# Where the weights are split: from GpSimd to ScalarE and VectorE, in a fused AdaLN block with linear attention and routed experts

## The chip, the cores and the metric

The kernel runs on one NeuronCore of a Trainium2 chip. The metric is the device time of one execution in microseconds (us). The kernel before was timed three times: 1975.85, 1978.46 and 1978.96 us, median 1978.46. The page and the trace come from one more, profiled execution.

## What is computed

x is 4096 tokens (2 sequences of 2048) by 512, all in float32. Cut to what matters, with `_rms`, `_layernorm`, `_silu` and `gelu` as usual:

```
sa, ca, ga, sb, cb, gb = (_silu(c) @ wmod)            # six rows per sequence; ga, gb kept away from zero
h = _layernorm(x) * (1 + ca) + sa
q, k, v = split(_rms(h) @ w_qkv.T);  q = _rms(q);  k = _rms(k);  w = exp(k)
y = sigmoid(q) * (cumsum(w * v) / (cumsum(w) + 1e-6))  # along the sequence
u, g = split(y @ w_swiglu.T)
x = x + ga * (h + u * silu(g) @ w_out.T)               # DFF = 2048
h = _layernorm(x) * (1 + cb) + sb
routed = top 2 of 8 experts of gelu(h @ w1 + b1) @ w2 + b2, softmax gates, H = 256
shared = gelu(h @ shared_w1 + shared_b1) @ shared_w2 + shared_b2
x = x + gb * (routed + shared)
```

## The kernel before

It is written by hand, engine by engine: five instruction streams (`@block.sync` for the DMA queue SP, `gpsimd`, `tensor`, `scalar`, `vector`), each executed in the order in which it is written, tied together by semaphores. A `wait_ge` holds all that stands behind it on its engine.

Every large product is float32 in three passes: an operand is held as a high part (`fp32r`) and a low part (the rest), and TensorE adds hi·hi, hi·lo and lo·hi (`product` L685 to L688, `by_tokens` L690 to L693). So each weight, too, is fetched raw and split once: a copy that rounds (hi), then a subtraction raw - hi (lo). The weights come in 36 pieces, numbered in the order of use: pieces 0 to 3 are w_qkv, split in six halves on ScalarE and VectorE (`weights_hi`, `weights_lo`); B0 = 4 to 11 and C0 = 12 to 19 are the two halves of the first feed-forward, 128x1536 each; S0 = 20 to 23 the shared expert's and R0 = 24 to 39 the routed experts', 128x1024 each. Pieces 4 to 39 are split by GpSimd in `split_piece` (L548 to L559) and fetched into two raw buffers in turn: pieces 4 to 7 by SP (`piece`), the others by GpSimd (`fetch`). `w_ok` counts pieces that are done. TensorE waits for it ahead of the first use of each; a piece takes the place of one that is no longer read, hence the waits on `dn` ahead of the splits.

The stages, in the words used below:

- **Stage A**, 32 groups of 128 tokens. For each group g TensorE does k (12 products), turns the next group's rows, `turn_group` (L720), then q (12 products), turns the last group's w, e and w·v (`sums`: L750, L754, L761), then v (12 products). VectorE does in the same loop (L1536 to L1558): `k_times_v(g-1)` (L1459), `quotient(g-2)` (L1501 to L1503), in every fourth group `roots` and `deviations`, then `columns_lo(g+1)` (L1434, which TensorE's next group waits for), `scales(g)` (L1442 to L1450, which wait for squares from ScalarE), `denominator(g-1)` (four scans, L1474, and L1478), `sum_kv(g-1)` (four scans, L1489), and `norm(g+4)` (L1406, L1417).
- **Stages b and c**, the first feed-forward in two passes over 8 tiles of 512 tokens. A tile has 8 blocks s: 24 products up (L686 to L688) and, two blocks later, 12 down (L691 to L693). ScalarE does silu (L1183) and hi (L1185) of a block, VectorE the product `s_t` (L1567) and lo (L1570); then VectorE has its hooks: in b, `token_stats` at s = 2 and `first_residual` (L1616 to L1620) at s = 3 to 6, in c the second norm and the router. After a tile come `x_lo` of the next (L1354, which TensorE waits for) and `evacuate` (L1629, L1633). TensorE can go up two blocks beyond the last block that VectorE has finished.
- **Stage s**, the shared expert, 8 tiles of 4 blocks; its low part is L1843. Between the blocks VectorE does the router of the last two tiles (`positions`, L1689 to L1703) and the tables of the experts.
- **Stage r**, 71 slots of 128 gathered rows, each through one expert. GpSimd gathers rows (L632) and adds results to `out` (L642). Ahead of the first slots VectorE finishes the last shared tile: `last_shared`, then `last_residual` (L1909) for four row groups, after which SP stores the tile, and `slot_o(0)` waits for that store (`out_st`) before it writes the first `o_t` (L1935).

GpSimd's order around the splits: pieces 4 to 7 in stage A, 8 to 11 from A's end on, 12 to 19 as b's last tile frees the places, then the router's writes (`to_lists`, L597) in turn with 20 to 35, the first gathers, 36 and 37, more gathers, 38 and 39.

Of the kernel before, what the change touches and what calls it, by code (L numbers as in the profile page):

```python
# [34 lines left out]
def build(nc, x_tok, c, wmod, w_qkv, w_swi, w_sh, w_exp, b1s, b1r, b2p, b2s, gate_w, ident, tri, rank, tokid, ebase,  # L35
# [48 lines left out]
    with ctx:  # L84
# [238 lines left out]
        def _(sp):  # L323
            def piece(i):

                sp.wait_ge(w_ok, max(i - 1, B0))
                src, _, _, n = piece_of(i)
                sp.dma_start(raw[i % 2][:, 0:n], src).then_inc(raw_in[i % 2], 16)

# [217 lines left out]
        def _(pool):  # L547
            def split_piece(i):  # L548
                _, hi, lo, n = piece_of(i)
                if i < SP_PIECES:  # L550
                    pool.wait_ge(raw_in[i % 2], 16 * (i // 2 - 1))
                else:
                    pool.wait_ge(raw_sw[i % 2], 16 * ((i - SP_PIECES) // 2 + 1))
                src = raw[i % 2][:, 0:n] if i < S0 else raw_4[i % 2][:, :]
                if i >= R0:
                    src = src.rearrange("p (m n) -> p m n", n=hi.shape[2])
                nc.gpsimd.tensor_scalar(hi, src, 1.0, 1.0, ALU.mult, ALU.mult).then_inc(w_hi_ok, 1)  # L557
                pool.wait_ge(w_hi_ok, i + 1)
                nc.gpsimd.tensor_tensor(lo, src, hi.bitcast(F32), ALU.subtract).then_inc(w_ok, 1)  # L559

            def fetch(i):
                pool.wait_ge(w_ok, i - 1)
                src, _, _, n = piece_of(i)
                pool.dma_start(raw[i % 2][:, 0:n] if i < S0 else raw_4[i % 2][:, :], src).then_inc(raw_sw[i % 2], 16)


            pool.wait_ge(w_ok, B0)
            for i in range(B0, B0 + 2):
                split_piece(i)

            split_piece(6)
            fetch(8)
            split_piece(7)
            fetch(9)
            pool.wait_ge(a.mm, 3 * NG)
            for i in range(8, C0):
                split_piece(i)
                fetch(i + 2)
# [6 lines left out]

            for j in range(NB):
                pool.wait_ge(ffn["b"].dn, NB * LAST + j + 1)
                split_piece(C0 + j)
                fetch(C0 + j + 2)
# [13 lines left out]
            for j, freed in enumerate((0, 1, 2, 2)):  # L603
                pool.wait_ge(ffn["c"].dn, NB * LAST + freed + 1)
                split_piece(S0 + j)
                fetch(S0 + j + 2)

            for i in range(R0, R0 + 4):
                pool.wait_ge(ffn["c"].dn, NB * LAST + (5 if i < R0 + 2 else 6))
                split_piece(i)  # L610
                fetch(i + 2)
# [1 line left out]
            for i in range(R0 + 4, R0 + 8):
                pool.wait_ge(ffn["c"].dn, NB * NT)
                split_piece(i)
                fetch(i + 2)

            pool.wait_ge(hT_st, 16 * NT)
            pool.wait_ge(n2.logit_mm, NT)
            pool.wait_ge(hr_st, 16 * NSUB * NT)  # L620
# [1416 lines left out]
```

## Time and profile before

| | |
|---|---|
| three runs, us | 1975.85, 1978.46, 1978.96 |
| the profiled execution, us | 1976.18 |
| its span in the trace, us | 1974.1 |
| TensorE busy | 97% |
| VectorE, ScalarE, GpSimd busy | 67%, 34%, 23% |
| TensorE's mean granted clock | 0.989 of full |
| tile period in b | 65.28 us |
| group period in A, undisturbed | 10.0 us |

The busy share of TensorE (PE) counts a product from issue to its modelled end, so neighbours overlap; what counts are the gaps, and the stretches at a lower granted clock. PEld is its weight load, DVE VectorE, ACT ScalarE, POOL GpSimd. Times are microseconds from the span's start. A line of the timeline has start, duration, engine, line, operation, tiles, shapes and count, and in brackets how long the engine had been idle and what ended that.

### The profile page before, as it was taken

Reading aid. Unit: us, or ns where it says so; the run is one execution under the profiler, and the core shown is the slowest. Engines: PE = TensorE matmul, PEld = TensorE weight load, DVE = VectorE, ACT = ScalarE, POOL = GpSimd, SP = SyncE. Lnnn points to the kernel's source line nnn. Section 1 sums busy time; section 2 is a strip of 40 time slices with the busy share of each in tenths; the row PEclk is TensorE's granted clock in tenths of the full one; section 3 lists DMA queues with packets and bytes.
Section 4 is the critical chain, followed back from the end, with each engine's and each line's share of the span. In section 5 each row is a group of like instructions: output and inputs, shape, how many; then the busy total and the mean of one; then the engine's idle time right before and its main releaser. Section 6 shows DMA issues by size and latency. Waiting matters only on the chain.

```text
span 1974.1 us, 26317 instructions
## 1 busy us (share of the span) xinstructions
PE 1915.7 (97%) x8850; PEld 1536.1 (78%) x8850; DVE 1315.2 (67%) x2728; ACT 665.5 (34%) x1376; POOL 444.2 (23%) x319
## 2 busy tenths in 40 slices
PE   6998999999999999998999999999999989899998
PEld 4677888878888888886887787787786767688886
DVE  5789999875545554567256356456458587488887
ACT  4666776421112111111112212212223333255554
POOL 0031000220000000035001011011062351588885
PEclk9999999999999999998999999999999999999999
DMA  5224110231110211034011321311234464488887
GB/s 187 99 91 142 54 54 27 68 116 65 64 45 21 75 64 53 12 112 155 22 65 54 98 66 59 114 67 59 93 119 170 141 193 156 147 155 154 154 153 107
DMA packets 86686, 189.96 MB, mean 96 GB/s; under 512 B 9525, under 2 KB 26198, under 8 KB 81516
## 3 DMA queue, kind: packets, MB, share of 16 engines
q1 hardware_dynamic: 63564, 130.92, 19.7%
q0 software_dynamic: 22992, 57.37, 14.0%
q8 instruction: 74, 1.21, 0.3%
q14 instruction: 56, 0.46, 0.1%
HBM read 118.56 MB, written 72.12 MB: 97 GB/s over the span
## 4 chain that ended last, share of the span: by engine, by line
PE 66%; DVE 8%; POOL 3%; issue 3%; ACT 1%; DMA 1%; POOLq 0%; DVEq 0%
PE bank L686 12%; PE bank L688 11%; PE bank L687 11%; PE bank L691 7%; PE bank L692 6%; PE bank L693 6%; PE bank L929 3%; POOL out L642 1%; PE bank L856 1%; PE bank L931 1%; PE bank L959 1%; PE bank L958 1%; PE bank L957 1%; PE bank L916 1%; POOL rows_t L632 1%
## 5 line engine op out<-in xcount | busy, mean ns | idle before, releaser
L686 PE MATMUL bank<-x_hi,w_blk 128*128 128x512 f32 x1024 | 404.5, 395 | 9.2 <-DVE x_lo L1354 5.4
L688 PE MATMUL bank<-x_hi,w_blk 128*128 128x512 f32 x1024 | 400.1, 391 | 0.0
L687 PE MATMUL bank<-x_lo,w_blk 128*128 128x512 f32 x1024 | 399.5, 390 | 0.0
L1567 DVE TENSOR_TENSOR s_t<-act_t,bank 128x512 f32<-128x512 f32 x128 | 87.8, 686 | 305.3 <-PE bank L688 305.0
L1185 ACT ACTIVATE s_hi<-s_t 128x512 fp32r<-128x512 f32 x128 | 80.9, 632 | 458.1 <-DVE s_t L1567 458.1
L686 PEld LDWEIGHTS bank<-x_hi,w_blk 128*128 128x128 f32 x1024 | 192.9, 188 | 51.4 <-DVE x_lo L1354 6.6
L688 PEld LDWEIGHTS bank<-x_hi,w_blk 128*128 128x128 f32 x1024 | 192.8, 188 | 40.9
L687 PEld LDWEIGHTS bank<-x_lo,w_blk 128*128 128x128 f32 x1024 | 193.1, 189 | 38.8
L557 POOL TENSOR_SCALAR w_blk<-raw 128x1536 fp32r<-128x1536 f32 x16 | 24.2, 1514 | 814.3 <-PE bank L693 663.6
L691 PE MATMUL bank<-w_blk,s_hi 128*128 128x512 f32 x512 | 200.7, 392 | 0.0
L693 PE MATMUL bank<-w_blk,s_lo 128*128 128x512 f32 x512 | 199.4, 389 | 0.0
L692 PE MATMUL bank<-w_blk,s_hi 128*128 128x512 f32 x512 | 199.3, 389 | 0.0
L1183 ACT ACTIVATE act_t<-bank 128x512 f32<-128x512 f32 x128 | 76.3, 596 | 354.5 <-PE bank L688 354.5
L597 POOL DMA_INDIRECT slot_list<-pay,pos x64 | 64.2, 1003 | 557.5 <-DVE pos L1703 540.1
L691 PE MATMUL bank<-w_blk,xc_hi 128*128 128x512 f32 x384 | 158.5, 413 | 6.0 <-DVE xc_lo L1434 4.8
L1570 DVE TENSOR_TENSOR s_lo<-s_t,s_hi 128x512 fp32r<-128x512 f32 x128 | 92.3, 721 | 89.5 <-ACT s_hi L1185 88.8
L693 PE MATMUL bank<-w_blk,xc_lo 128*128 128x512 f32 x384 | 151.7, 395 | 0.0
L692 PE MATMUL bank<-w_blk,xc_hi 128*128 128x512 f32 x384 | 151.0, 393 | 0.0
L642 POOL DMA_INDIRECT out<-o_t,ids_t x71 | 113.9, 1604 | 31.9 <-DVE o_t L1935 28.9
L691 PEld LDWEIGHTS bank<-w_blk,s_hi 128*128 128x128 f32 x512 | 96.1, 188 | 25.7 <-issue 6.2
L929 PE MATMUL bank<-w_all,xT_hi 128*128 x284 | 110.5, 422 | 5.3 <-issue 5.3
L693 PEld LDWEIGHTS bank<-w_blk,s_lo 128*128 128x128 f32 x512 | 96.1, 188 | 20.2
(264 smaller groups left out, 3637.5 us busy)
## 6 DMA issues: line engine op xcount, KB each, us to landing
x_t<-y_scratch SPq DMA_DIRECT2D x24, 1024.0 KB, 4.8
residual<-r_t SPq DMA_DIRECT2D x16, 1024.0 KB, 4.3
r_t<-residual SPq DMA_DIRECT2D x16, 1024.0 KB, 5.7
raw<-w_swi POOLq DMA_DIRECT2D x12, 768.0 KB, 4.6
y_scratch<-y_t SPq DMA_DIRECT2D x32, 256.0 KB, 2.6
r_t<-x_tok SPq DMA_DIRECT2D x8, 1024.0 KB, 5.3
h_rows<-hrow SPq DMA_DIRECT2D x32, 256.0 KB
y_scratch<-hT SPq DMA_DIRECT2D x8, 1024.0 KB, 3.9
```

Source lines behind the costliest of these rows:

```text
L642: pool.indirect_dma_start(out, bass.IndirectOffsetOnAxis(ap=ids_t[:, j:j + 1], axis=0), o_t[j % NO][:, :], None, compute_op=ALU.add).then_ ...
L686: nc.tensor.matmul(dst, w[:, 0, col:col + P], rhs_hi, start=start, stop=False)
L687: nc.tensor.matmul(dst, w[:, 0, col:col + P], rhs_lo, start=False, stop=False)
L688: return nc.tensor.matmul(dst, w[:, 1, col:col + P], rhs_hi, start=False, stop=stop)
L691: nc.tensor.matmul(dst, lhs_hi, w[:, 0, col:col + D], start=start, stop=False)
L692: nc.tensor.matmul(dst, lhs_hi, w[:, 1, col:col + D], start=False, stop=False)
L693: return nc.tensor.matmul(dst, lhs_lo, w[:, 0, col:col + D], start=False, stop=stop)
L929: nc.tensor.matmul(bank_u[j % 2][:, 0:2 * H], xT_hi[:, j % 2, tok], w_all[:, bass.ds(at_e + m * 2 * H, 2 * H)], start=(m == 0), stop=False)
L1183: nc.scalar.activation(act_t[:, s % 2, :], bank[4 + 2 * s % 3][:, :], ACT.Silu).then_inc(f.act_ok, 1)
L1185: nc.scalar.activation(s_hi[:, s % 3, :], s_t[:, s % 2, :], ACT.Copy).then_inc(f.sh_ok, 1)
L1567: nc.vector.tensor_tensor(s_t[:, s % 2, :], act_t[:, s % 2, :], bank[4 + (2 * s + 1) % 3][:, :], ALU.mult).then_inc(f.s_ok, 1)
L1570: nc.vector.tensor_tensor(s_lo[:, s % 3, :], s_t[:, s % 2, :], s_hi[:, s % 3, :].bitcast(F32), ALU.subtract).then_inc(f.sl_ok, 1)
```

## The change

GpSimd splits nothing any more; it only fetches, all 36 pieces. `piece_hi` is a copy on ScalarE, `piece_lo` the subtraction on VectorE, both placed by hand: pieces 4 to 7 in groups 8, 12, 16 and 20 of stage A; 8 to 11 in blocks 0 to 3 of b's first tile; 12 to 16 in blocks 3 to 7 of b's last tile, 17 to 19 in blocks 0 to 2 of c's first; 20 to 23 in blocks 3 to 6 of c's last; twelve in stage s (`S_TURNS`), two in its last block, two in slots 1 and 3. Two orders change beside that: `sums_kv` now stands behind the v products, and `sum_kv` a group later and ahead of `quotient`; and the last three `last_residual` stand behind the first slots' work.

```diff
-        late_rows = [o_t[4], o_t[5], p_t[0], p_t[1]]
+        late_rows = [p_t[0], p_t[1], o_t[4], o_t[5]]
...
+        def pieces_at(p, t, s):
+            if p == "b" and t == 0 and s < 4:
+                return (B0 + 4 + s,)
+            if p == "b" and t == LAST and s >= 3:
+                return (C0 + s - 3,)
+            if p == "c" and t == 0 and s < 3:
+                return (C0 + 5 + s,)
+            if p == "c" and t == LAST and 3 <= s < 7:
+                return (S0 + s - 3,)
+            if p == "s" and (t, s) == (LAST, 3):
+                return (R0 + 12, R0 + 13)
+            if p == "s" and (t, s) in S_TURNS:
+                return (R0 + S_TURNS.index((t, s)),)
+            return ()
+
+        S_TURNS = ((1, 1), (1, 2), (1, 3), (2, 1), (2, 3), (3, 0), (3, 2), (3, 3), (4, 2), (4, 3), (5, 0), (5, 2))
+
+        A_TURNS, R_TURNS = (8, 12, 16, 20), (1, 3)
...
-            if t == 5:
+            if t == 4:
                     gates_out(LAST)
...
-            def split_piece(i):
...
             def fetch(i):
-                pool.wait_ge(w_ok, i - 1)
...
+                pool.wait_ge(w_ok, max(i - 1, B0))
+                pool.dma_start(raw_of(i)[:, 0:piece_of(i)[3]], piece_of(i)[0]).then_inc(raw_sw[i % 2], 16)
...
                 ins.then_inc(a.cum, 1)
+
+            def sums_kv(g):
                 pe.wait_ge(a.kv_ok, g + 1)
...
                     sums(g - 1)
                 project(g, 2)
+                sums_kv(g - 1)
...
+            def piece_hi(i):
+
+                src, hi, _, n = piece_of(i)
+                act.wait_ge(raw_sw[i % 2], 16 * ((i - B0) // 2 + 1))
+                act.wait_ge(w_ok, max(i - 1, B0))
...
+                nc.scalar.activation(hi, from_, ACT.Copy).then_inc(w_hi_ok, 1)
...
+                if g in A_TURNS:
+                    piece_hi(B0 + A_TURNS.index(g))
...
+                        for i in pieces_at(p, t, s):
+                            piece_hi(i)
...
                 slot_o(j)
+                if j in R_TURNS:
+                    piece_hi(R0 + 14 + R_TURNS.index(j))
...
+            def piece_lo(i):
+
+                _, hi, lo, n = piece_of(i)
+                dve.wait_ge(w_hi_ok, i + 1)
...
+                nc.vector.tensor_tensor(lo, from_, hi.bitcast(F32), ALU.subtract).then_inc(w_ok, 1)
...
                 if g >= 2:
+                    sum_kv(g - 2)
                     quotient(g - 2)
...
                 denominator(g - 1)
-                sum_kv(g - 1)
...
                     norm(g + NSUB)
+                if g in A_TURNS:
+                    piece_lo(B0 + A_TURNS.index(g))
...
+                        for i in pieces_at(p, t, s):
+                            piece_lo(i)
...
             last_residual(0)
             slot_g(0)
-            for g in range(1, NSUB):
-                last_residual(g)
             for j in range(NSLOT):
...
                     slot_g(j + 1)
+                if j == 0:
+                    for g in range(1, NSUB):
+                        last_residual(g)
+                if j in R_TURNS:
+                    piece_lo(R0 + 14 + R_TURNS.index(j))
```

VectorE at the end of group 8 of stage A, before (rk_a ends `scales`; xr is `norm`, kv_t `k_times_v` of the next turn of the loop):

```order
L1450 SCALAR_TENSOR_TENSOR rk_a<-b_a,y_a 128x2
L1474 SCALAR_TENSOR_TENSOR W_t_55<-bank,W_t_54,tri_t 128x128 x4
L1478 SCALAR_TENSOR_TENSOR den_t_59<-bank,W_t_55 128x512
L1489 SCALAR_TENSOR_TENSOR kv_sum_57<-bank,kv_sum_56,tri_t 128x128 x4
L1391 TENSOR_TENSOR sqv<-sv_a 128x4
L1392 SCALAR_TENSOR_TENSOR sqv<-sqv,va_a 128x4
L1393 SCALAR_TENSOR_TENSOR rs_a<-sqv,sv_a 128x4
L1406 SCALAR_TENSOR_TENSOR xr<-xr,mv_a,gain_a_93 128x512
L1417 SCALAR_TENSOR_TENSOR xr<-xr,rs_a,shift_a_95 128x512
L1459 SCALAR_TENSOR_TENSOR kv_t_66<-bank,r_pair,w_t_64 128x512
L1501 TENSOR_TENSOR den_t_59<-den_t_59,rec_t 128x512
```

and of the change:

```order
L1469 SCALAR_TENSOR_TENSOR rk_a<-b_a,y_a 128x2
L1493 SCALAR_TENSOR_TENSOR W_t_55<-bank,W_t_54,tri_t 128x128 x4
L1497 SCALAR_TENSOR_TENSOR den_t_59<-bank,W_t_55 128x512
L1410 TENSOR_TENSOR sqv<-sv_a 128x4
L1411 SCALAR_TENSOR_TENSOR sqv<-sqv,va_a 128x4
L1412 SCALAR_TENSOR_TENSOR rs_a<-sqv,sv_a 128x4
L1425 SCALAR_TENSOR_TENSOR xr<-xr,mv_a,gain_a_93 128x512
L1436 SCALAR_TENSOR_TENSOR xr<-xr,rs_a,shift_a_95 128x512
L1383 TENSOR_TENSOR w_blk<-raw_83,w_blk 128x1536
L1478 SCALAR_TENSOR_TENSOR kv_t_66<-bank,r_pair,w_t_64 128x512
L1508 SCALAR_TENSOR_TENSOR kv_sum_57<-bank,kv_sum_56,tri_t 128x128 x4
L1520 TENSOR_TENSOR den_t_59<-den_t_59,rec_t 128x512
```

The four scans of kv_sum have moved behind the next kv_t, and the subtraction of piece 4 stands between the norm and kv_t.

VectorE at the first slots, before (r_t is `last_residual`, xT_lo the low part of a slot's turned rows, here of slot 3, gb_row and o_t are `slot_o(0)`):

```order
L1914 TENSOR_TENSOR gT_lo<-bank,gT_hi 128x256
L1909 TENSOR_TENSOR r_t<-r_t,o_t_139 128x512
L1909 TENSOR_TENSOR r_t<-r_t,p_t_147 128x512
L1909 TENSOR_TENSOR r_t<-r_t,p_t_148 128x512
L1919 TENSOR_LOAD tab
L1919 ISA x2
L1835 TENSOR_TENSOR xT_lo<-bank,xT_hi 128x512
L1898 ISA
L1898 TENSOR_TENSOR u_t<-bank,b1r_t 128x256
L1901 TENSOR_TENSOR u_t<-u_t,bank 128x256
```

and of the change, a few rows later (the xT_lo of slot 3 stands ahead of these, the one shown is slot 4's):

```order
L1927 TENSOR_TENSOR u_t<-u_t,bank 128x256
L1940 TENSOR_TENSOR gT_lo<-bank,gT_hi 128x256
L1935 TENSOR_TENSOR r_t<-r_t,p_t_148 128x512
L1935 TENSOR_TENSOR r_t<-r_t,o_t_138 128x512
L1935 TENSOR_TENSOR r_t<-r_t,o_t_139 128x512
L1945 TENSOR_LOAD tab
L1945 ISA x2
L1951 SCALAR_TENSOR_TENSOR gb_row<-gbd_t,late_t,gbs_t_114 128x512
L1963 TENSOR_TENSOR o_t_134<-p_t_147,gb_row 128x512
L1859 TENSOR_TENSOR xT_lo<-bank,xT_hi 128x512
```

Three residual additions now stand behind the work of slots 1 to 3, and directly ahead of `slot_o(0)`.

## Rows read from the trace of the kernel before

**Rows 1.** Stretches: from:to, length, busy of each engine, PEclk, DMA share, GB/s.
```profile
145.00:165.00 20.00, 15.89 (x75) 13.11 (x74) 18.27 (x37) 12.95 (x36) 4.31 (x3) 0.83 0.28 84
416.00:436.00 20.00, 17.59 (x78) 14.26 (x77) 15.62 (x38) 4.10 (x7) 0.00 (x0) 1.00 0.00 1
905.00:925.00 20.00, 14.57 (x47) 10.16 (x47) 19.34 (x13) 1.32 (x3) 14.76 (x8) 0.74 0.45 150
1596.00:1611.00 15.00, 10.60 (x35) 6.97 (x36) 7.35 (x17) 0.63 (x2) 11.72 (x11) 0.89 0.72 214
```
**Rows 2.** Timeline of PE: the longest waits, in A, b, s and r.
```profile
151.36 0.90 PE L761 MATMUL bank<-ident_t,kv_t 128*128 128x128 f32 x3 [4.11 <-DVE kv_t L1459]
...
420.30 0.47 PE L686 MATMUL bank<-x_hi,w_blk 128*128 128x512 f32 x1 [2.41 <-DVE s_t L1567]
...
1600.40 0.74 PE L691 MATMUL bank<-w_shr,s_hi 128*128 128x512 f32 x1 [4.52 <-DVE s_lo L1843]
...
1724.79 0.79 PE L929 MATMUL bank<-w_all,xT_hi 128*128 x1 [4.90 <-issue]
```
**Rows 3.** Timelines of POOL and DVE in b's last tile, of DVE in its first.
```profile
887.38 3.80 POOL L559 TENSOR_TENSOR w_blk<-raw,w_blk 128x1536 fp32r<-128x1536 f32 x1
...
887.75 3.72 DVE L1616 TENSOR_SCALAR tmp<-r_t,mv,rstd 128x512 f32<-128x512 f32 x1
...
421.46 0.54 DVE L1616 TENSOR_SCALAR tmp<-r_t,mv,rstd 128x512 f32<-128x512 f32 x1
```
**Rows 4.** Groups by line and form: splits on POOL, DVE and ACT.
```profile
L559 POOL TENSOR_TENSOR w_blk<-raw,w_blk 128x1536 fp32r<-128x1536 f32 x16 | 59.6, 3727 | 1.4
...
L1361 DVE TENSOR_TENSOR w_blk<-raw_q,w_blk 128x1024 fp32r<-128x1024 f32 x6 | 7.2, 1222 | 2.8 <-ACT w_blk L1051 2.8
...
L1051 ACT ACTIVATE w_blk<-raw_q 128x1024 fp32r<-128x1024 f32 x6 | 6.0, 1050 | 1.5 <-DMA raw_q<-w_qkv 1.5
```
**Rows 5.** Timeline of PE in A: the turns of the rows of groups 8, 15 and 31.
```profile
120.00 0.60 PE L720 MATMUL bank<-ident_t,xr 128*128 128x128 f32 x4
...
202.49 0.60 PE L720 MATMUL bank<-ident_t,xr 128*128 128x128 f32 x4
...
362.98 0.60 PE L720 MATMUL bank<-ident_t,xr 128*128 128x128 f32 x4
```
**Rows 6.** Timeline of DVE in A: k_times_v (L1459) of groups 19, 20, 22 and 30, start of scales(30).
```profile
263.75 0.74 DVE L1459 SCALAR_TENSOR_TENSOR kv_t<-bank,r_pair,w_t 128x512 f32<-128x512 f32 x1
...
275.95 0.74 DVE L1459 SCALAR_TENSOR_TENSOR kv_t<-bank,r_pair,w_t 128x512 f32<-128x512 f32 x1
...
294.62 0.75 DVE L1459 SCALAR_TENSOR_TENSOR kv_t<-bank,r_pair,w_t 128x512 f32<-128x512 f32 x1
...
367.17 0.23 DVE L1442 TENSOR_SCALAR u_a<-ms_a,r_a 128x2 f32<-128x2 f32 x1 [1.67 <-ACT junk L1089]
...
372.25 0.72 DVE L1459 SCALAR_TENSOR_TENSOR kv_t<-bank,r_pair,w_t 128x512 f32<-128x512 f32 x1
```
**Rows 7.** Timeline of PE: first products of b's tiles 6 and 7, and c's tile 1.
```profile
776.75 0.39 PE L686 MATMUL bank<-x_hi,w_blk 128*128 128x512 f32 x1
...
842.03 0.39 PE L686 MATMUL bank<-x_hi,w_blk 128*128 128x512 f32 x1
...
982.19 0.39 PE L686 MATMUL bank<-x_hi,w_blk 128*128 128x512 f32 x1
```
**Rows 8.** Timeline of DVE in b's first tile: s_t of blocks 2 and 3.
```profile
404.05 0.69 DVE L1567 TENSOR_TENSOR s_t<-act_t,bank 128x512 f32<-128x512 f32 x1 [3.42 <-PE bank L688]
...
419.47 0.69 DVE L1567 TENSOR_TENSOR s_t<-act_t,bank 128x512 f32<-128x512 f32 x1
```
**Rows 9.** Timeline of DVE in r: residuals 2 and 3, slot 3's xT_lo, the first o_t.
```profile
1719.73 4.26 DVE L1909 TENSOR_TENSOR r_t<-r_t,p_t 128x512 f32<-128x512 f32 x2
1723.92 0.68 DVE L1835 TENSOR_TENSOR xT_lo<-bank,xT_hi 128x512 fp32r<-128x512 f32 x1
...
1728.50 0.69 DVE L1935 TENSOR_TENSOR o_t<-p_t,gb_row 128x512 f32<-128x512 f32 x1 [1.52 <-DMA out<-r_t]
```

More of the change, by code:

```diff
@@ L244, in build @@
         wmod_in = [sem(f"wmod_in{v}") for v in range(3)]
-        raw_in = [sem(f"raw_in{i}") for i in range(2)]
         part_in = [sem(f"part_in{k}") for k in range(3)]
@@ L323, in _ @@
         def _(sp):
[L324 to L328, printed above, removed]
             def load_part(k):
@@ L547, in _ @@
         def _(pool):
-            def split_piece(i):
[L549 to L559, printed above, removed]
-            def fetch(i):
-                pool.wait_ge(w_ok, i - 1)
[L563 to L578, printed above, removed]
+            def fetch(i):
+                pool.wait_ge(w_ok, max(i - 1, B0))
+                pool.dma_start(raw_of(i)[:, 0:piece_of(i)[3]], piece_of(i)[0]).then_inc(raw_sw[i % 2], 16)
+            pool.wait_ge(a.tr_ok, NSUB + 2)
+            for i in range(B0, C0 + 2):
+                fetch(i)
             pool.wait_ge(y_st, 16 * NG)
@@ L584, in _ @@
             pool.dma_start(steps_t[:, :, :], steps.rearrange("p (k e) -> p k e", k=2)).then_inc(sc_st[3], 16)
[L586 to L589, printed above, removed]
+            for i in range(C0 + 2, S0 + 2):
+                fetch(i)
             def to_lists(u):
@@ L602, in _ @@
                 to_lists(u)
[L603 to L611, printed above, removed]
-            to_lists(LAST - 1)
[L613 to L620, printed above, removed]
+            for i in range(S0 + 2, R0 + 6):
+                fetch(i)
+            to_lists(LAST - 1)
+            for i in range(R0 + 6, R0 + 8):
+                fetch(i)
+            to_lists(LAST)
             for i in range(R0 + 8, R0 + 10):
-                split_piece(i)
-                fetch(i + 2)
-            to_lists(LAST)
+                fetch(i)
             AHEAD = 3
@@ L651, in _ @@
                 bass.IndirectOffsetOnAxis(ap=blk_t[0:NSLOT, 0:1], axis=0)).then_inc(lb_in, 16)
-            pool.wait_ge(g_st, 16 * NT)
-            for i in range(R0 + 10, R0 + 12):
-                split_piece(i)
-                fetch(i + 2)
+            for i in range(R0 + 10, R0 + 14):
+                fetch(i)
             pool.wait_ge(lb_ok, 1)
@@ L663, in _ @@
                 gather(j)
-            pool.wait_ge(ffn["s"].dn, NB_S * LAST + 2)
-            for j in range(2):
-                split_piece(R0 + 12 + j)
-                fetch(R0 + 14 + j)
+            for i in range(R0 + 14, R0 + 16):
+                fetch(i)
             pool.wait_ge(ffn["s"].dn, NB_S * NT)
@@ L672, in _ @@
                 gather(j)
-            for j in range(2):
-                split_piece(R0 + 14 + j)
             for j in range(AHEAD):
@@ L890, in _ @@
                             sums(NG - 1)
+                            sums_kv(NG - 1)
                         if s >= 2:
@@ L1265, in _ @@
                     block_s(t, s)
+                    for i in pieces_at("s", t, s):
+                        piece_hi(i)
                     if s == 2:
@@ L1884, in _ @@
                         order_of_additions()
+                    for i in pieces_at("s", t, s):
+                        piece_lo(i)
                 if t == LAST:
```

32 lines of the change are left out of this document (29 added, 3 removed).

## The prediction

> **What bounds the kernel now.** I read the page first: TensorE is busy nearly all of the span, so only what it waits for, and what it does at half clock (1.2 of 2.4 GHz), can be won. Next its longest waits, in time [rows 2]: they stand in few places, and each is ended by VectorE (the 4.90 us "issue" too: that product needs slot 3's xT_lo, which VectorE ended at 1724.60 [rows 9]). Then VectorE and GpSimd side by side at such a place. The reader is to see that in b's last tile L1616 takes 3.72 us and ends 0.3 us after GpSimd's subtraction, while in b's first tile, without GpSimd, it takes 0.54 [rows 3]. GpSimd holds VectorE for the length of its own instruction. The stretches then give the clock: it was 0.83, 0.74 and 0.89 of full around the waits that follow such holds, and 1.00 after the 2.41 us wait at 420 [rows 1]. The last view is VectorE's own pace in stage A, since that is where the change adds work to an engine with little room.
>
> **Prices.** GpSimd's subtraction of 128x1536 took 3.73 us. On VectorE 128x1024 took 1.22, on ScalarE the copy 1.05 [rows 4]. VectorE's 128x512 took 0.69 [rows 8], so 512 elements more are 0.53, and a 128x1536 piece is 1.76 us there (estimate), and about 1.5 on ScalarE. Added in all: 16 x 1.76 + 20 x 1.22 = 52.6 us on VectorE, 45 on ScalarE. ScalarE is idle most of the time, and I cost its copies at nothing: in A each stands ahead of a wait on VectorE's deviations, in b and c behind the block's own hi. If that cover were gone, each would add up to 1.5 us to the subtraction behind it. Each copy also brings waits, for the raw data and for the place in memory; behind them stand the next block's silu and hi, and behind those VectorE. The raw data are asked for two pieces ahead, which is two blocks (16 us in b), and a place is free one block ahead, so I count no wait. Fetching costs nothing either: GpSimd now has nothing else to do there, and the four fetches taken from SP leave its queue shorter. `gates_out` one tile earlier holds SP's next loads of x and r only until ScalarE's first block of that tile; TensorE needs them a tile later.
>
> **Stage A.** Lost before: TensorE's turns of groups 8 and 15 are 82.5 us apart [rows 5], seven undisturbed groups take 70.0; 12.5 us, of which the 4.11 us wait and 3.4 us of half clock (17% of 20 us) are most [rows 1, 2]. Some 0.5 us more fall in small waits later. After: VectorE's loop took 12.20 us in group 20 (with roots) and 9.33 in the next two [rows 6], so four groups 40.2 against TensorE's 40.0. With a piece it is 42.0: 2.0 us too long in each of four rounds. What can be absorbed? I measure VectorE's lead by how long after L720 its loop starts. It can be late by 2.6: `columns_lo` then ends 3.2 (kv_t, three quotient steps and xc_lo, 0.6 to 0.7 each) + 1.5 (four scans, about 0.4 each, that now stand ahead) later, at the 7.3 after L720 when the next group's products begin (10.0 less twelve products of 65.28 / 288 = 0.227 [rows 7]). It cannot be earlier than -0.8: scales(30) began 4.2 after L720 and the loop went on 5.1 later [rows 5, 6], less 1.5 of scans, plus 1.4 of norm. A round with a piece pushes the loop 12.20 + 1.76 - 10.0 = 3.96 later, the three groups after it take 2.0 back. From -0.8 that gives 3.2, 0.6 over; in each later round 0.6 + 3.96 is 2.0 over. Waits: 0.6 + 3 x 2.0 + 2 x 0.2 = 7.0. **Gain 13.0 - 7.0 = 6.0.** The moved turn of w·v takes a wait away (that for kv_t, 4.11 us), but it is `xc_lo` that is late next. Bounds: 13.0 (all hidden) and, with half clock behind the three 2.0 us waits, 6.0 - 3 x 1.7 = 0.9.
>
> **Start of b.** Before, block 3's s_t came 15.4 us after block 2's, with all hooks between and no GpSimd in the way for most of it [rows 8], and TensorE waited 2.41. After, block 2 starts earlier (no holds in the quotient, which were some 6 us), but piece 9 waits for ScalarE: two table loads, the reciprocal and the copy put its end at about 402.2 instead of 404.05; then 15.4 + 1.76 for piece 10: block 3's s_t at 419.4, as before. TensorE, no longer late ahead of it, waits some 3.6 us in one go instead of 2.4. The time is equal; but the clock stayed full after 2.41 and fell after 4.11 [rows 1, 2]; 3.6 is nearer to 4.11. **Cost 1.7** (3.4 us at half), bounds 0 and 3.4. Here the Trainium skill speaks against the change: "TensorE: Matmul & The Clock Gate", section "What's actually happening", says the gate follows how busy TensorE has been, whatever it waited for. By it the three 2.0 us waits in A might cost clock too; and the sum would be 3 x 1.7 higher, 1961; by the row of the 2.41 us wait they don't, and I go by the row.
>
> **b's last tile to c's first.** Tiles take 65.28 us; from tile 7's start to c's second it was 140.16 instead of 130.56 [rows 7]: 9.6 lost, as the four x_lo were held behind pieces 17 to 19, at a clock of 0.74 [rows 1]. After, VectorE has in a block of 8.2 us: 2.0 for the block, 2.7 of residual, 1.76: 6.4. In block 7 the piece and four x_lo (2.5) end about 7.4 us after the last up product, c's first begins 8.2 after. Nothing waits. **Gain 9.6**; the lower bound 7.9, if 1.7 of it becomes wait. The fetches now follow `w_ok` two pieces later, 16 us, and would have to land that late to matter.
>
> **Stage c to s.** The chain at 1490 to 1530 (last c tile, second norm, store and load of r_t) has no GpSimd in it: nothing.
>
> **Stage s.** The wait of 4.52 us at 1600 and 1.65 us of clock (11% of 15 us) [rows 1, 2] come from `positions` on VectorE, which GpSimd held while it split pieces 29 to 31 (11.7 us busy in those 15). After, one piece (1.2 us) lies ahead of it in that tile; without the holds, and this piece added, VectorE reaches block 2's s_lo some 4 us ahead of need. **Gain 6.2.** The other ten pieces have room.
>
> **Stage r.** TensorE waited 4.90 for xT_lo of slot 3, held by three residuals, of which the last two alone took 4.26 beside GpSimd [rows 2, 9]. These now follow, so slot 3 is on time. What is late next: `slot_o(0)` waits for the store of the last tile, which took 4.5 us from the last residual (1723.99) to 1728.50 [rows 9], and slot 4's xT_lo is queued behind it on VectorE. With slot 3's xT_lo, a u and a gT_lo ahead (to 1719.6) and three residuals of 0.65 without holds they end at about 1721.6, the store at 1726.1, o_t and slot 4's xT_lo at 1727.4; TensorE is there at 1723.3 and waits 4 us. Its slot takes 3.45. Then piece 38 makes slot 5 some 1 us late, piece 39, whose copy waits for slot 3's down products, makes slot 7 2.5 us late: it starts at about 1741, where it did before. **Gain 0**, bounds 3.4 (one slot less late) and -2.
>
> **Sum.** -6.0 + 1.7 - 9.6 - 6.2 + 0 = -20.1 us against the profiled execution's 1976.2: 1956.1. The median shown is 2.3 higher, so **1958** for a median of runs.
>
> **Rivals.**
> - *The new waits halve the clock.* Three waits of 2.0 in A, one of 3.6 in b, one of 4 in r: five falls of 1.7 instead of one, up to 7 us more: 1965. For it: that the clock fell at all four kinds of place; against: full clock after 2.41 [rows 1].
> - *More is hidden.* VectorE catches up in A and TensorE waits there for little (up to 7 us), no fall in b (1.7), slot 4 on time (3.4): 1946 to 1952. For it: VectorE idles 1 us in every fourth group for ScalarE, which the later place could cover; against: that idle time hangs on deviations, which stay behind the moved scans.
> - *VectorE only changes what holds it.* A piece held VectorE 3.2 + 0.4 us in b's last tile [rows 3] and now costs 1.76; if copies and waits for them eat the rest, nothing is won: 1976 to 1980. "Perfetto Trace Analysis", section "Optimizing Scalar/DVE Operations" in the Trainium skill, says that moving work between these two engines might not help as they share a port; the row has twice the price for the hold.
> - *Slower: VectorE becomes the bound.* If every added subtraction is on TensorE's path, 52.6 us come against 13.0 + 9.6 + 6.2 and at most 11 in r and at b's start won: +13, 1991. It decides where a block's own work on VectorE leaves under 1.8 us. In A it does already (40.2 of 40.0); in b (6.4 of 8.2) it doesn't. The whole of b, c and s would have to behave like A.
>
> **Chances.** Forecast 0.58 (by its bounds 1952 to 1962), halved clock 0.16, more hidden 0.16, no change 0.05, slower 0.05. Half of the no-change case lies within 0.2% (4 us, about what a measurement of this kernel tells from none). Faster 0.92, same 0.03, slower 0.05. The range 1947 to 1968 takes in most of both neighbours and leaves some 15 in 100 out.
>
> **What would show it.** Right: no first_residual step over 0.75 us; undisturbed groups 8 to 23 of A with waits for xc_lo (not kv_t) of about 2 us in groups 9, 13, 17 and 21; no wait at b's last x_lo; b's first tile about 70.6 us as before; one wait of 4 us before slot 4. Wrong: a 128x1536 subtraction well off 1.76, ScalarE's hi waiting for raw data, half clock inside A, or TensorE's waits moved into c or s.

## The result, and the profile after

The changed kernel takes 1964.51 us (median of five, 1963.55 to 1968.42) against 1977.04 for the kernel before beside it (five, 1975.33 to 1978.96). The ratio is **0.9944, 95% interval 0.9930 to 0.9958**: 12.5 us faster. The forecast was 1958 (1947 to 1968), some 20 us faster. The direction and the range held; 8 us of the gain are missing, and the views say where.

First the page of the profile after: its span and the engines' busy time.

```profile
span 1962.7 us, 26330 instructions
PE 1913.0 (97%) x8850; PEld 1535.2 (78%) x8850; DVE 1282.6 (65%) x2764; ACT 706.0 (36%) x1412; POOL 279.5 (14%) x251
```

GpSimd is down from 23% to 14%. VectorE has 36 more instructions (one for each piece) and yet a smaller share (67% before): what the holds had added to its busy time is gone. Where the time went is told by the same event in both traces:

| us from the span's start | before | after | ahead |
|---|---|---|---|
| A: turn of group 8's rows | 120.00 | 119.25 | 0.8 |
| A: turn of group 31's rows | 362.98 | 365.20 | -2.2 |
| b: first product | 379.76 | 382.08 | -2.3 |
| b: first product of tile 7 | 842.03 | 844.87 | -2.8 |
| c: first product of tile 1 | 982.19 | 975.43 | 6.8 |
| s: first product | 1489.49 | 1482.80 | 6.7 |
| s: first product of tile 3 | 1578.73 | 1570.97 | 7.8 |
| s: first product of tile 4 | 1610.69 | 1595.94 | 14.8 |
| r: turn of slot 4's rows | 1719.30 | 1704.27 | 15.0 |
| r: turn of slot 9's rows | 1744.17 | 1732.55 | 11.6 |
| span | 1974.1 | 1962.7 | 11.4 |

So A costs 3.0 us where 6.0 were to be won, and r costs 3.4 where nothing was; b to c gives 9.6 and s's fourth tile 7.0. The stretches of [rows 1] again, and three more of A (columns as there):

```profile
145.00:165.00 20.00, 18.01 (x92) 14.62 (x91) 19.33 (x45) 13.33 (x36) 0.00 (x0) 1.00 0.29 93
190.00:210.00 20.00, 18.01 (x84) 14.66 (x85) 19.33 (x44) 13.38 (x35) 0.00 (x0) 0.91 0.26 85
235.00:255.00 20.00, 18.50 (x89) 15.33 (x89) 19.14 (x45) 14.12 (x36) 0.00 (x0) 0.91 0.21 63
280.00:300.00 20.00, 19.53 (x93) 16.07 (x94) 19.06 (x45) 14.71 (x38) 0.00 (x0) 0.91 0.18 53
416.00:436.00 20.00, 17.34 (x71) 13.92 (x70) 17.12 (x37) 4.84 (x7) 3.33 (x6) 0.91 0.24 83
905.00:925.00 20.00, 20.00 (x90) 16.57 (x89) 14.98 (x20) 7.79 (x11) 1.06 (x2) 1.00 0.59 203
1596.00:1611.00 15.00, 15.00 (x67) 12.44 (x67) 14.33 (x27) 7.01 (x11) 0.00 (x0) 1.00 0.72 248
```

At 905 and 1596 TensorE (first busy time) is now full, at full clock. In A three stretches out of four read 0.91: some 3.4 us at half clock in each, which loses 1.7. Such a stretch is called a fall below. TensorE's waits, to be held against [rows 2]:

```profile
148.77 0.50 PE L656 MATMUL bank<-w_blk,xc_hi 128*128 128x512 f32 x1 [1.99 <-DVE xc_lo L1453]
...
192.54 0.66 PE L656 MATMUL bank<-w_blk,xc_hi 128*128 128x512 f32 x1 [1.99 <-DVE xc_lo L1453]
...
421.72 0.77 PE L651 MATMUL bank<-x_hi,w_blk 128*128 128x512 f32 x1 [2.66 <-DVE s_t L1589]
...
1712.65 0.79 PE L898 MATMUL bank<-w_all,xT_hi 128*128 x1 [4.33 <-issue]
...
1727.87 0.49 PE L898 MATMUL bank<-w_all,xT_hi 128*128 x1 [1.97 <-issue]
```

There are four of 1.99 in A (148.77, 192.54, 236.50, 280.47), for `xc_lo` and not for `kv_t`, as forecast; behind the first there is no fall, behind the others there is one each. What makes VectorE late there is one view further, its timeline in group 8, which holds a piece:

```profile
128.46 0.74 DVE L1478 SCALAR_TENSOR_TENSOR kv_t<-bank,r_pair,w_t 128x512 f32<-128x512 f32 x1
...
133.53 0.17 DVE L1443 TENSOR_SCALAR var_t<-ss_a 128x4 f32<-128x4 f32 x1 [0.70 <-ACT junk L1068]
134.16 0.16 DVE L1410 TENSOR_TENSOR sqv<-sv_a 128x4 f32<-128x4 f32 x1 [0.47 <-ACT sv_a L1081]
...
142.07 1.75 DVE L1383 TENSOR_TENSOR w_blk<-raw,w_blk 128x1536 fp32r<-128x1536 f32 x1
143.74 0.74 DVE L1478 SCALAR_TENSOR_TENSOR kv_t<-bank,r_pair,w_t 128x512 f32<-128x512 f32 x1
```

and ScalarE's at the same time:

```profile
131.40 1.48 ACT L1053 ACTIVATE w_blk<-raw 128x1536 fp32r<-128x1536 f32 x1
132.78 0.62 ACT L1068 ACTIVATE junk<-xr 128x512 f32<-128x512 f32 x1
...
133.85 0.21 ACT L1081 ACTIVATE sv_a<-sv_a 128x4 f32<-128x4 f32 x1
```

The subtraction takes 1.75 us, as estimated from [rows 4, 8]. But the piece's copy (L1053) stands in ScalarE's queue ahead of the sum of squares (L1068) and the root (L1081) that `roots` on VectorE needs, and VectorE idles 0.70 + 0.47 us that it doesn't idle in group 24, which has roots and no piece. From one `kv_t` to the next (L1478) a loop takes 15.28 us in group 8, 15.26 in 12, 16 and 20, 12.41 in group 24, and 9.51 in most others (9.26 to 10.01 in groups 15, 17 to 19 and 23). **A round of four groups takes VectorE 43.8 us, not 42.0**; TensorE needs 40.1. VectorE can't make up for that within a round, so TensorE loses the difference.

In r VectorE's timeline shows two kinds of idle time, one for the store, two for ScalarE's copies of pieces 38 and 39:

```profile
1706.41 0.75 DVE L1951 SCALAR_TENSOR_TENSOR gb_row<-gbd_t,late_t,gbs_t 128x512 f32<-128x512 f32 x1
1711.16 0.69 DVE L1963 TENSOR_TENSOR o_t<-p_t,gb_row 128x512 f32<-128x512 f32 x1 [4.00 <-DMA out<-r_t]
1711.77 0.68 DVE L1859 TENSOR_TENSOR xT_lo<-bank,xT_hi 128x512 fp32r<-128x512 f32 x1
...
1715.24 1.23 DVE L1383 TENSOR_TENSOR w_all<-raw,w_all 128x1024 fp32r<-128x1024 f32 x1 [1.67 <-ACT w_all L1053]
...
1724.46 1.23 DVE L1383 TENSOR_TENSOR w_all<-raw,w_all 128x1024 fp32r<-128x1024 f32 x1 [1.68 <-issue]
...
1726.99 0.68 DVE L1859 TENSOR_TENSOR xT_lo<-bank,xT_hi 128x512 fp32r<-128x512 f32 x1
```

Slot 4's xT_lo (1711.77) and slot 7's (1726.99) end what TensorE waits for.

### The profile page after: what moved, and what is told of

Same layout as the page of the kernel before. It is cut to its first block, busy times and chain, and to the rows that moved or that the text cites. A ratio compares the mean times of both kernels' runs of the same rounds, so it can differ in the third digit from the quotient of the medians.

```text
span 1962.7 us, 26330 instructions
## 1 busy us (share of the span) xinstructions
PE 1913.0 (97%) x8850; PEld 1535.2 (78%) x8850; DVE 1282.6 (65%) x2764; ACT 706.0 (36%) x1412; POOL 279.5 (14%) x251
## 4 chain that ended last, share of the span: by engine, by line
PE 75%; DVE 5%; issue 3%; POOL 3%; DMA 1%; ACT 0%; POOLq 0%; DVEq 0%; SPq 0%
PE bank L651 12%; PE bank L653 12%; PE bank L652 12%; PE bank L656 9%; PE bank L658 8%; PE bank L657 8%; PE bank L898 2%; POOL out L615 2%; PE bank L824 1%; PE bank L900 1%; PE bank L926 1%; PE bank L928 1%; PE bank L927 1%; PE bank L885 1%; POOL rows_t L605 1%
## 5 line engine op out<-in xcount | busy, mean ns | idle before, releaser
L651 PEld LDWEIGHTS bank<-x_hi,w_blk 128*128 128x128 f32 x1024 | 192.6, 188 | 42.7 <-DVE w_blk L1383 3.0
L656 PE MATMUL bank<-w_blk,xc_hi 128*128 128x512 f32 x384 | 161.0, 419 | 12.5 <-DVE xc_lo L1453 11.4
L563 POOL DMA_DIRECT2D raw<-w_swi x16 | 8.7, 547 | 909.7 <-DVE w_blk L1383 823.8
L658 PEld LDWEIGHTS bank<-w_blk,s_lo 128*128 128x128 f32 x512 | 96.1, 188 | 20.1
```

What stands on the lines that cost most here:

```text
L651: nc.tensor.matmul(dst, w[:, 0, col:col + P], rhs_hi, start=start, stop=False)
L656: nc.tensor.matmul(dst, lhs_hi, w[:, 0, col:col + D], start=start, stop=False)
L658: return nc.tensor.matmul(dst, lhs_lo, w[:, 0, col:col + D], start=False, stop=stop)
```

## Experiments

All are edits of the changed kernel unless said otherwise, each timed against the kernel before on the same chip. "8 to 31" is the time between TensorE's turns of groups 8 and 31 in A: 242.98 before, 245.95 after. "A round" is four of VectorE's loops in A, from one group with roots to the next, for example group 12's to 15's.

**The pieces of A in groups 27 to 30.**

```diff
-        A_TURNS, R_TURNS = (8, 12, 16, 20), (1, 3)
+        A_TURNS, R_TURNS = (27, 28, 29, 30), (1, 3)
```

> The change, with the four pieces of stage A in groups 27 to 30 (where norm is gone or going) instead of 8, 12, 16 and 20. Theory: in groups 8 to 23 VectorE's loop has no room, so the pieces there are what TensorE waits for (4 x 1.99 + 0.58 + 0.38 = 8.9 us) and what lets the clock fall behind three of the waits (3 x 1.8 = 5.4 us). Without them groups 8 to 26 should have periods of 10.0 us with no wait for xc_lo over 0.7, and full clock. Stage b starts at 382.08 - 11 to 14 = 368 to 371 us; total 1964.5 - 11 to 14 = 1951 to 1954 us. Rival 1: the moved turn of w times v with its scans ahead of columns_lo is what makes xc_lo late, pieces or not: waits of over 1 us stay in groups 9 to 26, total over 1959. Rival 2: GpSimd's transfers or the piece itself only move the wait to groups 27 to 31: the same 9 us there, total 1962 to 1966.

Measured: 1958.47 us, ratio 0.9912 [0.9893, 0.9931]. 8 to 31 takes 234.4 us, 11.5 less; the largest wait in groups 9 to 27 is 0.45, the clock full. So the pieces cost A what was said. But 5 us come back: VectorE reaches b's first x_lo, and behind it `scales(31)`, late; ScalarE's last e, which TensorE waits for ahead of b (`we_ok`), ends at 377.06, and b's first product starts at 377.15 after a wait of 3.39 us, with a fall of the clock behind. b's first tile takes 72.85 us instead of 71.11. The theory is right in A, and rival 2 for almost half of what is won there; the total lies between the two.

**One group later.** `A_TURNS` is (9, 13, 17, 21).

> The change, with the pieces of stage A in groups 9, 13, 17 and 21, one group behind those with roots and deviations. The excess per four groups stays 2.0 us (42.0 of work against 40.0), but it comes to the limit in two places: the group with the piece is 1.09 over, the one with roots 2.2 less the 1.34 won back in two groups = 0.86. Theory: two waits of about 1.1 and 0.9 us per round instead of one of 1.99, the sum as before. If the length of one wait decides about the clock (as the rows of before seemed to say: none behind 2.41, but a fall behind 4.11), these are short and no stretch at half clock is left in groups 9 to 24: 3 x 1.8 = 5.4 us less, total 1959. Rival, the fall goes by how little TensorE has done lately, waits however split: the stretches stay, total 1964 to 1965.

Measured: 1960.15 us, ratio 0.9923 [0.9906, 0.9941]. The waits are split (0.83 and 1.0 to 1.5), and the clock is 1.00 all through A (one of its stretches):

```profile
190.00:210.00 20.00, 18.47 (x96) 15.16 (x95) 19.43 (x40) 14.53 (x38) 0.53 (x1) 1.00 0.25 80
```

The number came out within 1.2 us, but not by the reason given. VectorE's four rounds are 43.2, 43.2, 42.7 and 43.2 us instead of 43.8, 44.0, 44.0 and 44.0 (from its `kv_t`), and 8 to 31 is 4.0 us shorter, where three falls fewer would be 5.1: what TensorE loses is nearly what VectorE's rounds are longer than 40.1, *with or without falls of the clock*. VectorE's work alone is 43.8 us a round in the change (15.26 + 3 x 9.51), paid by TensorE with 2.0 us of waiting and 1.7 of half clock; here 43.2 is paid with waits alone. Most of the gain is the copy no longer ahead of `roots` (12.35 + 11.81 against 15.26 + 9.51, 0.6 a round).

The falls add little of their own: 0.2 us in the rounds of groups 12 and 20, and 0.6 in that of group 16, where VectorE's work is only 43.4 and it idles 0.61 for ScalarE. Another run agrees: r_copy_ahead, below, has the change's stage A, and there the falls came in the first three rounds and not in the fourth. Its rounds are 43.98, 43.98, 43.99 and 43.76, the change's 43.81, 43.95, 43.97 and 44.00: the same round is 0.2 shorter without a fall.

**The old order of w times v.** The turn of w·v behind e again, `sum_kv(g - 1)` behind `denominator(g - 1)`:

```diff
                 project(g, 2)
-                sums_kv(g - 1)
...
-                    sum_kv(g - 2)
...
                 denominator(g - 1)
+                sum_kv(g - 1)
```

(and the turn back in `sums`).

> The change, with the turn of w times v and its scans back where they were (turned behind e, scanned in the same group), all splits on ScalarE and VectorE as in the change. It prices the moved turn where VectorE has the pieces. Theory: VectorE's loop is the same length, so the 2.0 us per round stay; but TensorE now asks for kv_t earlier (about 3 us after sums begin instead of behind the next twelve products), and waits for kv_t instead of xc_lo. The sum of waits stays near 9 us, with those for kv_t in the place; total 1964 to 1968. Rival 1: the later scans ahead of columns_lo cost and the old order is better: total under 1962. Rival 2: the moved turn is worth several us: total over 1970.

Measured: 1964.45 us, ratio 0.9947 [0.9928, 0.9966]; 8 to 31 246.24 against 245.95. The waits are for `kv_t`, 2.5 to 3.0 us. As forecast, the moved turn is worth nothing here. But two things cancel. VectorE's loop without piece or roots is 9.31 in the old order and 9.50 in the new, so the new one spends 0.2 us a group. And in the old order a fall is not nearly free: the first round, which has none, takes 43.3 us, the three with one 44.3 to 44.4, with VectorE idle for ScalarE in between. That falls cost little in A holds for the new order alone.

**The kernel before with the moved turn alone.**

> The kernel before, with nothing but the moved turn of w times v and the scans a group later; all later splits stay on GpSimd. Theory: the wait of 4.11 us for kv_t at 151.36 came of GpSimd's holds (4 instructions of 3.7 us), which stay; VectorE is as late, and xc_lo is late in its place, by less, as the limit for xc_lo lies 1.5 to 2 us later: a wait of 2 to 3 us and 3.4 us or no half clock: 1 to 4 us less than before, 1973 to 1976. Rival 1: the turn alone takes the whole 12.5 us stall away: 1964 to 1966. Rival 2: no effect or a loss: 1977 or more.

Measured: 1977.53 us, ratio 1.0009 [0.9998, 1.0020]; 8 to 31 takes 244.73 against 242.98. The wait for `kv_t` became waits for `xc_lo` and `kv_sum` (2.09, 2.65, 1.57). Rival 2: no effect or a small loss. The moved turn gains nothing in either setting.

**The last residual additions back ahead of the slots.**

```diff
             slot_g(0)
+            for g in range(1, NSUB):
+                last_residual(g)
             for j in range(NSLOT):
...
-                if j == 0:
-                    for g in range(1, NSUB):
-                        last_residual(g)
```

> The change, with the three last residual additions back ahead of the loop over the slots (their order as before). It prices their move. Theory: they put slot 3's xT_lo 2.0 us later (three of 0.65), TensorE waits 2 us for it; the store of the last tile starts 3.5 us earlier, so that slot 4's xT_lo is no longer late by 4.33 but on time. Slot 3 waits 1.5 to 2.5 us, slot 4 under 1; with one stretch at half clock less the stage is 2 to 5 us shorter than in the change: total 1960 to 1963. Rival: the move of the additions is worth what it was made for: a wait of 4 us or more before slot 3, total 1965 to 1968.

Measured: 1965.25 us, ratio 0.9940 [0.9924, 0.9957]. In the trace r, from the first turn of rows to slot 9's, is 41.2 us against 43.5, but the median doesn't show it, and misses both ranges. TensorE waits 0.38 before slot 3, 2.81 before slot 4, 0.70 before 5, 2.06 before 7. The profiled execution reached b's first product 2.8 us later than the change's (384.83), so its span can't show the 2.4 us either. Neither the expected wait before slot 3 came nor the rival's: without GpSimd's holds the additions were no longer what made slot 3 late, and moving them was not needed.

**slot_o(0) behind slot 4's xT_lo.**

```diff
-                if j >= 1:
+                if j >= 2:
                     slot_o(j - 1)
...
                     slot_g(j + 1)
+                if j == 1:
+                    slot_o(0)
```

> The change, with VectorE's slot_o(0) (which waits for the store of the last tile) behind slot 4's xT_lo, slot 3's u and slot 2's gT_lo instead of ahead of them. Theory: the wait of 4.33 us before slot 4's up product is only this place in VectorE's queue: it goes, with the 6.8 us at half clock behind it (3.4 us lost). Later slots start 6 to 8 us earlier, up to what slot 7's 1.97 us wait takes up; total 1956 to 1959. Rival 1: the store is needed in any case, as o_t's late start makes gates, p_t or the banks late: the wait moves one slot on, total 1963 to 1965. Rival 2: it is ScalarE that is late there; nothing changes.

Measured: 1960.59 us, ratio 0.9919 [0.9903, 0.9936]; r is 39.3 us against 43.5. The wait of 4.33 is 0.67; slot 5 waits 2.56 (two `slot_o` and piece 38 are now ahead of its xT_lo), slot 7 1.29, and a fall of 3.4 us is left. A place in VectorE's queue, as the theory has it, and part of it moves on: the total lies 1.6 us above the theory's range and below rival 1's.

**ScalarE's last two copies ahead of its slot_o.**

```diff
-                slot_o(j)
                 if j in R_TURNS:
                     piece_hi(R0 + 14 + R_TURNS.index(j))
+                slot_o(j)
```

> The change, with ScalarE's copies of pieces 38 and 39 ahead of slot_o(1) and slot_o(3) instead of behind them. Theory: VectorE waits 1.67 and 1.68 us for these copies with the later slots' subtractions behind it, and this is most of the 1.97 us wait before slot 7: that wait falls under 0.7, with the 3.4 us stretch at half clock behind it gone: 2 to 3.5 us less, total 1961 to 1962.5. Rival: piece 39's subtraction itself (1.23 us) in a slot of 3.45 us is too much, the wait stays over 1.5 us: total 1964 to 1965.

Measured: 1962.21 us, ratio 0.9933 [0.9917, 0.9950]; r is 41.2 us. The wait before slot 7 is 1.25 with the clock full, 2.4 us less in r: between theory and rival in the wait, the theory's in time.

**Stage c's subtractions on GpSimd.** In this run and the next three, work on the pieces goes back to GpSimd, to see what its holds cost; a hold is the time by which a VectorE instruction is longer beside one of GpSimd's. Here `piece_lo` of pieces 12 to 19 is left to GpSimd, behind ScalarE's copy as in the change.

> The change, with the subtractions of stage c's eight pieces (split from b's last tile into c's first) on GpSimd, their copies still on ScalarE. It tells whether the 9.6 us between b's last tile and c's second come of GpSimd holding VectorE. Theory: one GpSimd subtraction of 3.7 us per block of 8.2 us holds VectorE for its length wherever they meet; at b's last blocks the residual rows and x_lo take up to 3.7 us each again, c's first tile starts late: of the 9.6 us 3 to 9 come back: total 1968 to 1974. Rival: with the copy on ScalarE GpSimd has half its former work, keeps up, and the holds fall in VectorE's idle time: total 1964 to 1966; then it was GpSimd's lateness and not the hold.

Measured: 1966.49 us, ratio 0.9952 [0.9935, 0.9969]. The theory falls, and the rival's total is met within 0.5 us, though not by its reason. VectorE *is* held: in each of b's last blocks an addition of 0.69 us runs until GpSimd's instruction of 3.80 us ends, and so does the first x_lo:

```profile
882.02 3.87 DVE L1652 TENSOR_TENSOR r_t<-r_t,b_t 128x512 f32<-128x512 f32 x1
...
906.49 5.39 DVE L1373 TENSOR_TENSOR x_lo<-x_t,x_hi 128x512 fp32r<-128x512 f32 x4 [1.20 <-ACT x_hi L1024]
```

and TensorE doesn't notice: b's last tile and c's first take 65.28 us each.

**The whole split of those pieces on GpSimd**, each as soon as b frees the place, as before.

> The change, with both halves of the split of stage c's eight pieces on GpSimd, each as soon as b's block has freed the place, as before the change. With c_lo_on_gpsimd it tells what the 9.6 us at the border of b and c hang on: there the subtraction alone was on GpSimd, it held VectorE for 3.2 us in each of b's last blocks, and the tiles kept 65.28 us. Theory A, what counts is how many of GpSimd's instructions fall into one tile border: here a piece takes GpSimd 6.2 us (1.5 copy, 3.8 subtraction, 0.6 fetch, gaps), the last three follow one another without a break over c's first x_lo and the residual, and the 9.6 us come back (66.2 and 74.0 us for b's last and c's first tile, with half clock of 5 us and more): total 1972 to 1975. Theory B, the place in ScalarE's queue of the change (no hold) had nothing to do with it, and the gain came from the fetches asked for later or SP's shorter queue: total 1963 to 1967.

Measured: 1973.08 us, ratio 0.9988 [0.9977, 0.9998]. The tiles take 66.19 and 74.33 us: the loss of before is back, with its waits and its clock (VectorE's four x_lo in 12.62 us; TensorE's stretch at 905, at a clock of 0.85 where it was 0.74 before):

```profile
907.84 12.62 DVE L1376 TENSOR_TENSOR x_lo<-x_t,x_hi 128x512 fp32r<-128x512 f32 x4
```

```profile
905.00:925.00 20.00, 13.64 (x48) 9.80 (x47) 19.25 (x12) 3.32 (x6) 17.58 (x9) 0.85 0.42 152
```

GpSimd's three last subtractions start at 907.46, 913.76 and 920.00: it has fallen behind and works them off over the four x_lo, each held in its turn. One hold fits in a block; three in a row over the four x_lo don't.

**Four subtractions of stage s on GpSimd** (pieces 28 to 31, copies as in the change).

> The change, with the subtractions of four of the experts' pieces (28 to 31, in the third and fourth tile of stage s, around positions) on GpSimd, copies still on ScalarE, each in the block where it is now. By what c_lo_on_gpsimd showed: single subtractions of GpSimd spread over blocks (2.35 us each here) hold VectorE for their length, but cost TensorE nothing where VectorE has that much room. Theory: the fourth tile has 4 us of room, two or three holds of 1.1 to 1.7 us net each fit in: at most 1 us of the 7.0 us comes back, s tile 4 stays under 26 us, total 1964 to 1966. Rival: the chain of positions is so tight that holds lengthen it: tile 4 takes 27 to 32 us again, total 1967 to 1971.

Measured: 1964.08 us, ratio 0.9940 [0.9923, 0.9956]; the fourth tile takes 24.98 us. As the theory has it.

**Six whole pieces of stage s on GpSimd**, 28 to 33, in a row ahead of the last tile's lists, as before.

> The change, with both halves of the split of pieces 28 to 33 back on GpSimd, one after the other between the lists of the last two tiles, where they stood before the change. With s_lo_on_gpsimd (four subtractions on GpSimd, each in its own block: nothing lost) it tells what the 7.0 us of stage s's fourth tile hang on. Theory: as at the border of b and c, not a hold by itself but a row of them without a break: six times 1.1 us of copy, 2.3 to 2.7 of subtraction, 0.6 of fetch lie over positions and gates on VectorE (some 12 us of 28 held), the wait of 4 to 4.5 us for s_lo in the fourth tile and its stretch at half clock come back, the tile takes 30 to 32 us instead of 24.97: total 1969 to 1972. Rival: the gain in that tile came from what the change did elsewhere (gates stored a tile earlier in SP's queue, stage s beginning 7 us earlier relative to nothing else): the tile stays at 25 us, total 1964 to 1965.

Measured: 1969.99 us, ratio 0.9966 [0.9952, 0.9979]. The fourth tile takes 31.60 us (31.96 before), with the wait and the stretch of before:

```profile
1592.43 0.80 PE L668 MATMUL bank<-w_shr,s_hi 128*128 128x512 f32 x1 [4.93 <-DVE s_lo L1885]
```

```profile
1587.00:1602.00 15.00, 10.07 (x36) 6.46 (x34) 11.22 (x16) 1.25 (x3) 12.09 (x10) 0.89 0.63 232
```

**All that was learned, in one kernel**: `slot_o(0)` and the copies moved as above, and

```diff
-        A_TURNS, R_TURNS = (8, 12, 16, 20), (1, 3)
+        A_TURNS, R_TURNS = (5, 9, 28, 29), (2, 3)
```

> The change, improved by what the runs so far say: stage A's pieces in groups 5, 9, 28 and 29 (none in a row where roots already use up the room, none with b's first x_lo behind it), slot_o(0) behind slot 4's xT_lo as in r_store_behind, the last two pieces behind slots 2 and 3 with ScalarE's copies ahead of its slot_o. Theory: A loses one or two waits under 1.2 us and no clock instead of 8.9 us and three falls, its groups 8 to 27 have periods of 10.0 to 10.7; stage b starts 8 to 11 us earlier than in the change, measured from the first turn; stage r's waits before slots 4 to 7 are all under 1.5 us and the clock stays full there, 4 to 7 us less than the change. Together 12 to 17 us: total 1948 to 1953. Rival 1: gains in A only move to the start of b (as in a_late, 3.4 us before b's first product): 1953 to 1957. Rival 2: in r VectorE has no room left (3.2 of 3.45 us per slot), the lateness of 2.5 us of pieces and of the store must be paid whatever the order: r gains no more than r_store_behind's 3.9 us.

Measured: **1950.94 us, ratio 0.9881 [0.9863, 0.9898]**, 25 us faster than before, twice the change's gain.

```profile
span 1948.3 us, 26330 instructions
PE 1904.5 (98%) x8850; PEld 1528.8 (78%) x8850; DVE 1281.3 (66%) x2764; ACT 704.5 (36%) x1412; POOL 278.9 (14%) x251
```

The total is the theory's. 8 to 31 takes 235.81 us (10.1 less) with waits of 1.49 and 0.85 and no fall, and b's first product waits 1.25. Stage r to slot 9 takes 39.3 us, 4.3 less and no more than moving `slot_o(0)` alone: rival 2 holds there. Two of its waits are over the 1.5 us that the theory allowed, and behind the first the clock falls (timeline):

```profile
1703.84 0.78 PE L898 MATMUL bank<-w_all,xT_hi 128*128 x1 [2.32 <-issue]
...
1714.81 0.49 PE L898 MATMUL bank<-w_all,xT_hi 128*128 x1 [1.83 <-issue]
```

## Why the prediction was right in direction and too large

- **Stage A, -6.0: the failed step.** Forecast waits of 7.0 us and no lost clock; measured 8.9 of waits (4 x 1.99 + 0.58 + 0.38) and three falls of 3.4 us at half clock: A lost 13.0 before and 16 after. The step is in the paragraph on prices: "ScalarE is idle most of the time, and I cost its copies at nothing". The condition was named ("if that cover were gone"), the cover was taken to be a wait on VectorE's deviations, but behind the copy stands also the sum of squares that `roots` reads. VectorE idles 1.17 us more for it, and its loop is 1.1 longer in each of four rounds (15.26 against 12.41 + 1.75). A second, smaller term: the loops without piece are 9.51, not 9.33, since the moved scans cost 0.2, and the one with roots 12.41, not 12.20; 0.75 a round. With 43.8 us a round instead of 42.0, three rounds lose 4.0 to 4.5 us each (with small waits and groups of 10.03 for 10.0) where 2.0 were forecast, and the first 3.3 instead of 0.6. Of the 9.0 us between forecast and measurement some 4.4 are the copies, 3.0 the longer loops, 1.0 what the falls cost of their own, and the rest TensorE's groups of 10.03 (an estimate from these figures).
- **The clock in A.** The rival "the new waits halve the clock" came nearest in number, 1965, and three of the falls came where it had them; half clock inside A was also one of the forecast's signs of being wrong. But the number is in part luck: in A the falls cost 1.0 us of their own and not 5.1, and most of what is missing there is the copies and the longer loops, which the rival didn't have. The length of a wait was not enough as a measure: behind a single wait of 1.99 us the clock fell three times out of four in this trace. The Trainium skill ("TensorE: Matmul & The Clock Gate", section "What's actually happening") says the gate follows how busy TensorE has been. The forecast set the row of 2.41 against it, and three of the four waits in A went the page's way; why the fourth, of the same length, did not, no run here shows.
- **Start of b, +1.7.** The place and the fall were right (0.91 around 2.66 us), but the wait grew by 0.25 us instead of 1.2, and the tile took 71.11 instead of 70.59: +0.5 of the 1.7. What gave the rest back stays open.
- **b to c, -9.6.** Exactly that (the stretch at 905 against [rows 1]); no first_residual step takes over 0.69 us where [rows 3] has 3.72, and VectorE idles 1.77 us before each of the tile's later s_t. The reason was half right: c_lo_on_gpsimd and c_both_on_gpsimd show that it is not the hold as such but GpSimd's backlog of them over the four x_lo.
- **c to s, 0.** The two tiles together took 62.4 instead of 63.5, for a shorter stretch at half clock (3.4 against 6.8 us). That is chance and no gain of the change: at the same place r_old_residuals had 6.8 us and r_copy_ahead none, with the code up to there unchanged.
- **Stage s, -6.2.** Measured -7.0. Again a row of holds, not one, is what had cost it.
- **Stage r, 0: the second failed step**, mis-sized by 3.4. The wait for the store (4.00 us on VectorE, as reckoned from [rows 9]), the one before slot 4 (4.33, forecast 4) and the one before slot 7 (1.97, forecast 2.5) were there; the falls of the clock behind both (6.8 and 3.4 us at half, 5.1 lost) were not in the sum. Before there were 3.4 lost beside the wait of 4.90. The wait of 1 us forecast before slot 5 didn't come, which hid a part of the miss. And a part is ScalarE again: VectorE waits 1.67 and 1.68 us for the copies, and with these moved ahead r was 2.4 us shorter (r_copy_ahead).
- **Sum.** Won before group 8 0.8 us, in A -3.0, to b's tile 7 -0.6, b to c 9.6, c -0.1, s's first three tiles 1.1, the fourth 7.0, to slot 4 0.3, r's start -3.4, the rest -0.2: 11.4 us of span (rounded), against 20.1 forecast. Two terms of the sum were met (b to c, stage s); A and r were not, and the 1.1 us of s's first tiles is chance.
- **The rival that VectorE becomes the bound** held for A's groups 8 to 23, and in no other stage: its test (a loop with less than a piece's time left) was the right one.

## What to carry over

An engine that is idle two thirds of the time still isn't free: what costs is the instruction right behind the new one in its queue, and who waits for that. Look for each place of an added copy, not at the share. Where the other engine's loop is the longer one over a round, count the round's excess; waits and lost clock are only two ways of paying it. And a hold by GpSimd is cheap while it is one per block, dear when several are worked off in a row over what TensorE needs next.
